# Turning half of a mixer's x tiles with VectorE blocks and DMAs instead of TensorE

## The reference, cut to what matters

```
proj = x_norm @ in_proj_w.T                  # gate 8192, x 8192, B 1024, C 1024, dt 128 columns
xBC  = silu(causal_conv4(xBC) + conv_b)
x    = xBC[..., :8192] as 128 heads of 64;  B, C: 8 groups of 128
scores[i, j] = (C_i . B_j) * exp(cum_i - cum_j) * dt_j       for j <= i, per head
y    = scores @ x + D * x                    # per head, 256 rows of a sequence
g    = y * silu(gate);  g = g * rsqrt(mean(g*g in its group) + eps) * norm_w
out  = g @ out_w.T
```

## Time and profile before

| | us |
|---|---|
| median of 3 runs (lowest, highest) | 1899.85 (1897.21, 1901.18) |
| the profiled execution, its own time | 1896.68 |
| its span, first to last instruction | 1894.9 |
| busy in the span: TensorE matmuls | 1809.5 (95%) |
| GpSimd | 1438.4 (76%) |
| VectorE | 1343.9 (71%) |
| ACT | 1165.4 (61%) |
| TensorE in the chain that ended last | 79% |

### The profile page before, as it was taken

One profiled execution on the slowest core, in us unless ns is written; L12 is line 12 of the kernel. 1 busy time (PEld: TensorE's weight loads), 2 busy tenths in 40 slices (PEclk: granted clock), 3 DMA queues, 4 the chain that ended last, 5 costly groups with the idle time before them and its releaser, 6 DMA issues.

```text
span 1894.9 us, 29249 instructions
## 1 busy us (share of the span) xinstructions
PE 1809.5 (95%) x10780; PEld 1449.3 (76%) x10780; DVE 1343.9 (71%) x1701; ACT 1165.4 (61%) x2107; POOL 1438.4 (76%) x1435
## 2 busy tenths in 40 slices
PE   6998897989999999999999999999999999999977
PEld 4776675767888888888888887888888888888866
DVE  5654575676767867687678767777777687678656
ACT  3222433378766676777577667675777676676752
POOL 4312335479997998799789978997999799979972
PEclk9997998999999999999999999999999999999999
DMA  3000001032321222222222223222222122222201
GB/s 112 1 2 23 2 2 60 12 95 95 100 90 63 94 79 89 78 79 96 71 94 92 88 68 100 79 95 73 78 95 101 67 83 96 90 78 101 79 16 45
DMA packets 107025, 135.54 MB, mean 72 GB/s; under 512 B 9026, under 2 KB 74690, under 8 KB 106884
## 3 DMA queue, kind: packets, MB, share of 16 engines
q1 hardware_dynamic: 105924, 133.63, 21.5%
q10 hardware_dynamic: 960, 0.05, 0.0%
HBM read 131.02 MB, written 2.62 MB: 71 GB/s over the span
## 4 chain that ended last, share of the span: by engine, by line
PE 79%; DVE 2%; ACT 1%; issue 1%; POOL 0%; DVEq 0%; ACTq 0%; POOLq 0%
PE ps L146 20%; PE ps L148 20%; PE ps L147 20%; PE ps L2006 6%; PE ps L1961 3%; PE ps L2007 3%; PE ps L1099 2%; PE ps L2024 1%; PE ps L1989 1%; PE ps L118 1%; PE ps L2026 0%; DVE mix_u L1858 0%; DVE mix_xnT_lo L134 0%; DVE mix_xT L1731 0%; DVE mix_bT L1731 0%
## 5 line engine op out<-in xcount | busy, mean ns | idle before, releaser
L146 PE MATMUL ps<-mix_xnT_hi,mix_w_hi 128*128 128x512 f32 x1152 | 462.5, 401 | 0.8 <-ACT mix_ncum_rows L1669 0.7
L148 PE MATMUL ps<-mix_xnT_hi,mix_w_lo 128*128 128x512 f32 x1152 | 454.9, 395 | 0.0
L147 PE MATMUL ps<-mix_xnT_lo,mix_w_hi 128*128 128x512 f32 x1152 | 454.6, 395 | 0.0
L1731 DVE SCALAR_TENSOR_TENSOR mix_xT<-ps,mix_cur,mix_xT 128x510 f32<-128x510 f32 x378 | 279.2, 745 | 147.6 <-ACT mix_xT L1527 138.7
L1425 POOL TENSOR_SCALAR_AFFINE_SELECT mix_spread<-mix_spread 128x256 f32<-128x256 f32 x512 | 299.8, 620 | 0.0
L1751 DVE TENSOR_TENSOR mix_decay<-mix_decay,mix_cb 128x1536 f32<-128x1536 f32 x128 | 295.2, 2343 | 4.9 <-ACT mix_decay L1560 4.6
L1583 ACT ACTIVATE mix_g_hi<-mix_gated 128x512 fp32r<-128x512 f32 x128 | 81.0, 633 | 328.4 <-POOL mix_gated L1402 172.7
L148 PEld LDWEIGHTS ps<-mix_xnT_hi,mix_w_lo 128*128 128x128 f32 x1152 | 217.1, 188 | 50.7
L146 PEld LDWEIGHTS ps<-mix_xnT_hi,mix_w_hi 128*128 128x128 f32 x1152 | 217.4, 189 | 49.7 <-issue 1.2
L1558 ACT ACTIVATE mix_decay<-mix_spread,mix_cur_ncum 128x256 f32<-128x256 f32 x512 | 253.6, 495 | 0.0
L147 PEld LDWEIGHTS ps<-mix_xnT_lo,mix_w_hi 128*128 128x128 f32 x1152 | 217.5, 189 | 47.0
(11 more groups left out here) (274 smaller groups left out, 3329.8 us busy)
## 6 DMA issues: line engine op xcount, KB each, us to landing
mix_spread<-cum_rows SPq DMA_DIRECT2D x128, 512.0 KB, 4.0
mix_w_raw<-in_w_in_stream SPq DMA_DIRECT2D x144, 256.0 KB, 4.2
mix_wo_raw<-in_w_out_T SPq DMA_DIRECT2D x64, 256.0 KB, 3.6
att_w_raw<-in_w_attn_T SPq DMA_DIRECT2D x12, 256.0 KB, 4.1
x<-in_x SPq DMA_DIRECT2D x8, 256.0 KB, 4.4
out_rows<-x SPq DMA_DIRECT2D x8, 256.0 KB, 2.1
att_wp_raw<-in_w_proj_T SPq DMA_DIRECT2D x4, 256.0 KB, 2.8
mix_bT<-in_w_ffn_T SPq DMA_DIRECT2D x2, 512.0 KB, 4.8
```

The lines of the kernel that those rows point to most:

```text
L146: pe.matmul(out, lh, rh, start=(k == 0), stop=False)
L147: pe.matmul(out, lh, rl, start=False, stop=False)
L148: last = pe.matmul(out, ll, rh, start=False, stop=(k == tiles - 1))
L1731: dve.scalar_tensor_tensor(out=d[:, :, shift:T], in0=src[:, :, 0:T - shift], scalar=w[:, MK - 1 - shift:MK - shift], in1=d[:, :, shift:T], ...
```

## The change

TensorE turns the first four of the eight row tiles of a pair's x (`turn_x` with 2 instead of 4 tiles per half). Only the very first pair is still turned as before, with all eight. For the last four, VectorE makes two block transposes (`turn_blocks`: each 128 x 256, every 32 x 32 block turned in its place) from xT into the new buffer `blocked`, behind the skip of the pair before. A turned 128 x 128 tile also needs its blocks exchanged across partitions; `move_x` on SP does that with 16 DMAs per pair, each from 32 partitions of `blocked` to 32 partitions of x_dt, 4 tiles x 32 floats per partition. SP waits for both block transposes and for y of the pair before, and issues them behind the second spread load of the step. VectorE then scales the moved tiles by dt in place (`scale_moved`, two instructions of 128 x 256), ahead of `mix`, and `y_of_pair` waits for that too. The scaling of the tiles that TensorE turned is half as wide.

To make room in SBUF, the buffer `cur_ncum` goes, with the copy that filled it once per group (L1803); ACT's exponentials read their bias from `ncum_rows`. Some small buffers of the first masked layer and of the mixer's layer norm now lie in `blocked`, `mask_qk` and `ffn_stats`.

```diff
@@ SP
+            def move_x(pair):
+                sp.wait_ge(blocks_turned, 2 * pair)
+                sp.wait_ge(y_done, 2 * pair)
+                for i in range(P // STRIP):
+                    rows = slice(i * STRIP, (i + 1) * STRIP)
+                    strips = blocked[rows, :, :].rearrange("p t (q b) -> p t q b", b=STRIP)
+                    for q in range(P // STRIP):
+                        sp.dma_start(moved_x[q * STRIP:(q + 1) * STRIP, :, rows], strips[:, :, q, :])\
+                          .then_inc(moved, 16)
...
                     if more:
                         load_spread(g, k + 1, 1)
+                        move_x(PAIRS * g + k + 1)
@@ ACT
-                                   bias=cur_ncum[:, 2 * b, hc:hc + 1])
+                                   bias=ncum_rows[:, 2 * b, GHEADS * g + hc:GHEADS * g + hc + 1])
@@ VectorE
-            def scale_x(before, first_head):
+            def scale_x(before, first_head, tiles=2):
...
+            def scale_moved(pair, first_head):
+                dve.wait_ge(moved, 16 * MOVES * pair)
+                for half in range(2):
+                    tiles = slice(4 + 2 * half, 6 + 2 * half)
+                    x_rows = x_dt[:, tiles, :].rearrange("p t (h c) -> p t h c", c=MP)
+                    dtb = dt_rows[:, tiles, bass.ds(first_head, 2)]
+                    dve.tensor_tensor(x_rows, x_rows, dtb.unsqueeze(3).broadcast_to([P, 2, 2, MP]), ALU.mult)\
+                       .then_inc(moved_scaled, 1)
+
+            def turn_blocks(conv, buf):
+                dve.wait_ge(silu_x, conv + 2)
+                for half in range(2):
+                    at = 512 + half * 2 * P
+                    dve.transpose(blocked[:, 2 * half:2 * half + 2, :].rearrange("p t c -> p (t c)"), xT[:, buf, at:at + 2 * P])\
+                       .then_inc(blocks_turned, 1)
...
-                dve.tensor_copy(cur_ncum[:, :, :], ncum_rows[:, :, bass.ds(GHEADS * g, GHEADS)]).then_inc(cur_ready, 1)
...
+                    if pair:
+                        scale_moved(pair, GHEADS * g + 2 * k)
                     mix(g, k, 0)
                     mix(g, k, 1)
...
+                    if has_next:
+                        turn_blocks(n_conv(g, ("x", k + 1)), (k + 1) % 2)
@@ TensorE
-            def turn_x(uses, conv, buf):
+            def turn_x(uses, conv, buf, tiles=2):
...
-                    for j in range(4):
-                        t = 4 * half + j
+                    for j in range(tiles):
+                        t = tiles * half + j
...
                 pe.wait_ge(aux_free, x_ready(g, k, first))
+                at_least(pe, moved_scaled, 2 * pair)
```

More of the change, by code:

```diff
@@ L1164, in build_mixer @@
         square = sb("square", [P, ROWS])
+        blocked = sb("blocked", [P, NT // 2, P])
         squares = sb("squares", [P, ROWS])
@@ L1202, in build_mixer @@
         m.prob = flat(cb[:, :, :], "b c")[:, 0:NT * NCL].rearrange("p (t c) -> p t c", c=NCL)
-        m.row, m.best, m.best_c = sb("ffn_row", [P, 4, NT]), sb("ffn_best", [P, NCL]), sb("ffn_best_c", [NCL, 1])
-        m.chosen = sb("ffn_chosen", [NCL, P], BF16)
+        m.row, m.best, m.best_c = sb("ffn_row", [P, 4, NT]), blocked[:, 0, 0:NCL], sb("ffn_best_c", [NCL, 1])
+        m.chosen = sh.mask_qk[0:NCL, :]
         m.mask = xT[:, 0, 0:C]
@@ L1207, in build_mixer @@
         f = layer_parts(nc, sh, ins, "ffn1", m, fln, (0, 1), 2, (3, 4, 5, 0, 1, 2, 3, 5))
-        mln = build_layernorm(nc, sh, ctx, "mln", 6, into=(xnT_hi, xnT_lo), xn=xn)
-        lln = build_layernorm(nc, sh, ctx, "ffn2_ln", 0, into=(xnT_hi, xnT_lo), xn=xn)
+        mln = build_layernorm(nc, sh, ctx, "mln", 6, into=(xnT_hi, xnT_lo), xn=xn,
+                              kept=(blocked[:, 1, 0:NT * 6].rearrange("p (t n) -> p t n", n=6),
+                                    blocked[:, 2, 0:NT * 2].rearrange("p (t n) -> p t n", n=2)))
+        lln = build_layernorm(nc, sh, ctx, "ffn2_ln", 0, into=(xnT_hi, xnT_lo), xn=xn,
+                              kept=(sh.ffn_stats, sh.ffn_mv))
         last_layer = layer_parts(nc, sh, ins, "ffn2", m, lln, (2, 3), 7, (4, 5, 6, 2, 3, 7, 4, 5))
@@ L1229, in build_mixer @@
         tapped_c = [ap[:, n * 512:(n + 1) * 512] for ap in (gated[:, 1, :], square[:, :]) for n in range(2)]
+        blocks_turned, moved, moved_scaled = sem("blocks_turned"), sem("moved"), sem("moved_scaled")
+        STRIP, MOVES = 32, 16
+        moved_x = x_dt[:, NT // 2:NT, :]
         block = ctx.enter_context(nc.Block())
@@ L1711, in _ @@
             silu_gate(4, gated[:, 0, :], 4)
+            act.wait_ge(dt_out, 4)
             over_groups(body)
@@ L1733, in conv_taps @@
                                              op0=ALU.mult, op1=ALU.add).then_inc(convolved, 1)
-            def scale_x(before, first_head):
+            def scale_x(before, first_head, tiles=2):
                 for half in range(2):
                     dve.wait_ge(aux, before + half + 1)
[L1739 to L1742, removed]
+                    dtb = dt_rows[:, tiles * half:tiles * half + tiles, bass.ds(first_head, 2)]
+                    dve.tensor_tensor(x_dt[:, tiles * half:tiles * half + tiles, :].rearrange("p t (h c) -> p t h c", c=MP),
+                                      aux_bank(half)[:, 0:tiles * P].rearrange("p (t h c) -> p t h c", t=tiles, c=MP),
+                                      dtb.unsqueeze(3).broadcast_to([P, tiles, 2, MP]), ALU.mult).then_inc(aux_free, 1)
+            def scale_moved(pair, first_head):
[12 more added lines that the diff above has]
+                       .then_inc(blocks_turned, 1)
             def cur_w(item):
@@ L1801, in body @@
                 dve.tensor_copy(cur[:, :], consts[:, bass.ds(g, 1), :].rearrange("p a c -> p (a c)"))
[L1802 to L1803 removed]
+                dve.tensor_copy(cur_norm[:, :], norm_w[:, bass.ds(g, 1), :].rearrange("p a k -> p (a k)"))\
+                   .then_inc(cur_ready, 1)
                 dve.wait_ge(cur_ready, g + 1)
@@ L1818, in body @@
                     if k == 0 and first:
-                        scale_x(0, 0)
+                        scale_x(0, 0, 4)
                         take_cb(g, (0, 1))
@@ L2038, in body @@
                     if k == 0 and first:
-                        turn_x(0, 1, 0)
+                        turn_x(0, 1, 0, 4)
                     if k == 0:
```

3 lines of the change are left out of this document (1 added, 2 removed).

## The result

After the change the kernel takes 2155.62 us in the median (2151.59 to 2162.5, four runs) against 1900.51 (1897.21 to 1901.45, four runs) before. The ratio is 1.135 (95% interval 1.133 to 1.137): 255 us slower, where +121 was forecast. The profiled execution spans 2155.3 us.

The account below looks back on a forecast made before the run. TensorE (1392 of 1409 us) bound the kernel; then a two-step loop through SP's queue, 45.9 us, would. Eight groups at +13.6 and seven borders at +1.7 gave +121 us: 2021 us, range 1940 to 2220.

Parts of the forecast that it names:

- t: End of y's last skip (L1839) for a pair, the beat of the steps; a step took 20.57 us before.
- an issue far from 0.47 us: Sign against the forecast: SP's price per move; 0.47 us each was taken, 7.5 us for sixteen.
- a clock under 1.00: Sign against the forecast: TensorE's granted clock in the mixer's loop falling, which would point to rival 4.
- Rival 2: SP delays nobody; VectorE binds where it also adds rows to x (k = 2, 3): 1899 us, chance 0.04.
- The two-step loop: Through SP's queue, GpSimd, ACT, VectorE and TensorE: 12.5 + 12.9 + 20.5 = 45.9 us, against TensorE's 40.3.
- t to the first split: Block transposes 0.75, sixteen issues 7.5, weight landing 4.2: GpSimd gets its weights 12.5 us after t.
- GpSimd's chain to the gating: GpSimd's gapless work from a step's first split to the end of the second, ahead of gating y: 12.9 us.
- Gating to the end of the mixing: GpSimd's gating, ACT's g_hi, then VectorE's mixing: 16.2 less 0.3 plus 0.9 for new scalings, 16.8 us.
- End of the mixing to t: From VectorE's last mixing, which TensorE waits for, to the end of y's last skip: 3.7 us.
- rival 4: TensorE's clock falls after idling before y: 1.6 us lost three times a group, +38, 2059 us; chance 0.13.
- no bound of their own: Moved tiles land at 9.8 us after t; with scalings, mixing and y 19.4, under the 20.15 us step.
- Rival 3: SBUF to SBUF issues cost 0.81 us as in the attention; loop 51.4 us, total 2212 us, chance 0.22.

## Why the prediction was right and wrong

**Right.** The direction, and the mechanism: the moves' place in SP's queue, not their bytes, of which a quarter cost nearly as much (2140 us). The trace shows the path that was named: a block of issues with the weight load right behind it, GpSimd waiting for a DMA (359 us, 5.7 a step), the gating 4.7 us behind t, long and short steps in turn. The sizes of two of these signs were off: the block took 10.3 us and not 7 to 8, and the steps alternate near 22 and 28 and not near 22 and 24. Two signs that were named for being wrong came as well, an issue far from 0.47 us and a clock under 1.00. The exchange in SP's queue shows the mechanism by itself, 225 of 255 us. The step k = 1 was put at 21.9 and is 21.99. The gain of 0.42 us a pair is there wherever TensorE is the bound, and the removed copy and the narrower buffers cost nothing that the kernel without moves would show. Rival 2, 14 steps bound by VectorE and 1899 us in all, is what the kernels without moves and with hidden moves do: 1900.5 and 1899.6.

**Wrong: the size.** The two-step loop was put at 45.9 us; the one shown above takes 1006.43 - 955.91 = 50.5, and the mean of the 19 loops is 50.1. By its own terms:

- t to the first split: 970.04 - 955.91 = 14.1 (mean 14.5), forecast 12.5. The issues took 10.26 us instead of 7.5, and the split then began 3.1 us behind the load's issue, where 4.2 were allowed for the landing. The failed step is the choice of the piece count as what sets the price: the 0.47 is right for a source in DRAM (measured 0.475), and is 0.64 from SBUF, between the two bounds 0.37 and 0.81. The run from DRAM puts this price at 64 of the 134 us that the forecast missed; its total is still 71 us above the forecast.
- GpSimd's chain to the gating: 981.53 - 970.04 = 11.5 (mean 11.6), forecast 12.9. Late as it is, its subtraction and its masks no longer lie beside a mixing (1.29 and 1.49 us instead of 2.83 and 3.00; the subtraction at its short time had been an end of the range). The first split now does, and is 1.7 us longer.
- Gating to the end of the mixing: 1001.17 - 981.53 = 19.6 (mean 19.6), forecast 16.8. This is the largest failed term. The scalings were put at 0.9 and the mixes at 5.0, their time in the loop before; the delay pushed GpSimd's addition, subtraction and masks wholly beside them, and they took 2.16 and 6.69.
- End of the mixing to t: 1006.43 - 1001.17 = 5.3 (mean 4.4), forecast 3.7. Where y kept its speed it is 3.7 as forecast; the rest is the clock. It stood as rival 4 with a chance of its own, as if it were another case, at 1.6 us in each long step. In the step shown the price was right, but it was paid in 8 of 19 loops only, so 0.7 us in the mean belonged in the sum.

The four differences, +1.6, -1.4, +2.8 and +1.6, give the 4.6 us of this loop; for the mean loop it is 4.2. Over the groups behind the first, k = 1 to 7 take 172.0 us instead of the forecast 159.6, 27.1 more than before. The border is 4.2 us longer than before instead of 1.7: at the border from 1030.07 to 1068.72 TensorE waited 1.47 us for the first product's late weights, near the 1.25 that were forecast; what makes up the rest was not followed. The first group, which was taken like the others, goes up by 37.5 us. The sum is 7 x (27.1 + 4.2) + 37.5 = 257, near the 255 measured; the forecast had 13.6 us a group and 1.7 a border.

The moved tiles were said to be no bound of their own, at 19.4 us a step. With 0.64 us an issue this fails in part: in the short step shown VectorE waits 1.59 us for the last move, and the step takes 20.88 us instead of 20.15. It costs nothing there, as the gating at 981.53 comes later than that step's end.

Rival 3's price of 0.81 was too high for these moves, but its total, 2212, is nearer to the result than the forecast is, for another reason. It is also rival 3 that stretches the range to 2220, so that the range holds the result is luck. The transposes in blocks cost 0.42 us each, put at 0.37.

What stays open: why a source in SBUF makes an issue dearer, how the 92 us that the shortened addition gave back divide between the shorter chain and the undisturbed VectorE, since no run separates these two, and why the clock fell in some of the long steps and not in others.

## What to carry to other kernels

Before moving work into DMAs, count what each issue takes in its queue, by a row with the same kind of source, and look at what stands behind it: here two loads put ahead of the moves took 225 of 255 us back. Where a change makes an engine late, ask beside what its work will then lie; the durations of before hold only for the neighbours of before, and the gap it leaves on TensorE belongs in the sum with a share for the clock, not only among the rivals. And ask whether the engine that takes the work over has room in every step: VectorE's lack of it in two of eight steps cost the whole gain, and leaving out those two gave a kernel faster than both.

## What was not expected of the hardware

- An issue on SP's queue, back to back, took 0.64 us with SBUF as its source, with 32 or 128 pieces and on 32 or 128 partitions alike, and 0.475 us from DRAM with 128 pieces.
- VectorE's operations with both inputs in SBUF change their time with what GpSimd does: one mixing (128 x 1536) took 1.74 us at the least and 3.96 at the most in the changed kernel, a scaling (128 x 256) 0.41 to 2.63; GpSimd's four causal selections took 1.49 us alone and 3.00 beside the mixing. The scaling's and the mixing's rows, ns min/median/max, changed kernel:

```profile
L1769 DVE TENSOR_TENSOR mix_x_dt<-mix_x_dt,mix_dt_rows x126: 411/426/2633, 442.6 to 2078.8; 128x256 f32<-128x256 f32 x126
...
L1786 DVE TENSOR_TENSOR mix_decay<-mix_decay,mix_cb x128: 1745/2592/3959, 422.3 to 2080.8; 128x1536 f32<-128x1536 f32 x128
```

  The Trainium skill ("SBUF — State Buffer", "Who interferes with whom") says that a VectorE operation on two tensors in SBUF contends with a GpSimd operation that reads SBUF, over ports that only one of them holds at a time. These rows agree in kind: the maximum of 2.63 us is 2.2 us above the minimum, and one addition of GpSimd's took 2.59 us in the rows above. No run here shows which of the two had the ports when.
- A transpose of 128 x 256 floats in 32 x 32 blocks took 0.42 us of VectorE, with little spread (0.40 to 0.44).
